# Cross attention of a fused decoder: one operation fewer on the masked scores, the normalised rows written by ScalarE, the low parts of the experts' weights subtracted on GpSimd

## The reference, cut to what matters

```python
def _layernorm(x, axis=-1, eps=1e-05):
    m = jnp.mean(x, axis=axis, keepdims=True)
    v = jnp.var(x, axis=axis, keepdims=True)
    return (x - m) / jnp.sqrt(v + eps)

def _L0_xattn_ref(hidden_states, memory_tokens, memory_mask):
    B, S, D = hidden_states.shape                         # 8, 256, 512
    scale = 1.0 / jnp.sqrt(D)
    scores = jnp.einsum('bsd,bmd->bsm', hidden_states, memory_tokens) * scale
    scores = jnp.where(memory_mask[:, None, :], scores, -1e+30)
    attn = jax.nn.softmax(scores, axis=-1)
    readout = jnp.einsum('bsm,bmd->bsd', attn, memory_tokens)
    valid_b = jnp.any(memory_mask, axis=-1)
    return jnp.where(valid_b[:, None, None], readout, jnp.zeros_like(readout))

x = _layernorm(x + _L0_xattn_ref(x, ctx_2048, mask_BxS2_bk0))
x = _layernorm(x + _L0_ffn_ref(x, Wg, Wu, Wd, ...))       # the experts, next stage
...
```

## Time and profile before

| what | value |
|---|---|
| median of 3 runs | 1967.81 us (1967.73 to 1971.22) |
| the profiled execution | 1972.95 us, span 1971.2 us |
| PE busy | 1732.7 us (88%) |
| DVE busy | 1378.8 us (70%) |
| ACT busy | 1038.9 us (53%) |
| POOL busy | 595.4 us (30%) |

### The profile page before, as it was taken

How to read it: one execution, slowest core, us unless ns; L and a number is a source line. 1 busy time by engine, 2 the same in 40 slices (tenths; PEclk the granted TensorE clock), 3 DMA queues, 4 the chain that set the end, 5 groups by cost and what they waited for, 6 DMA issues and landing times. The chain is left out here.

```text
span 1971.2 us, 32220 instructions
## 1 busy us (share of the span) xinstructions
PE 1732.7 (88%) x11756; PEld 1344.6 (68%) x11774; DVE 1378.8 (70%) x2884; ACT 1038.9 (53%) x1936; POOL 595.4 (30%) x550
## 2 busy tenths in 40 slices
PE   4489999788869999999999997999998899968875
PEld 2255666424558999999999996888886677734443
DVE  8478888587945566665665665465665799749996
ACT  3426666645415444444444443565565354469993
POOL 6133332033110001000000002223333498945642
PEclk9669999957979999999999998999998899979998
DMA  5398998062502122222212233223225375100001
GB/s 170 38 100 97 93 98 98 4 206 66 195 35 65 57 68 65 82 68 63 76 57 78 68 110 105 102 97 129 76 85 151 88 175 134 39 0 11 22 22 32
DMA packets 148480, 163.87 MB, mean 83 GB/s; under 512 B 46240, under 2 KB 100384, under 8 KB 146528
## 3 DMA queue, kind: packets, MB, share of 16 engines
q1 hardware_dynamic: 143076, 151.85, 34.2%
q10 hardware_dynamic: 5248, 9.96, 1.4%
HBM read 116.86 MB, written 19.48 MB: 69 GB/s over the span
## 5 line engine op out<-in xcount | busy, mean ns | idle before, releaser
L1659 ACT ACTIVATE f_gate<-f_gu 128x256 f32<-128x256 f32 x264 | 98.6, 382 | 270.8 <-PE f_gu L1523 190.6
L1800 DVE TENSOR_TENSOR f_hid<-f_gate,f_gu 128x256 f32<-128x256 f32 x264 | 108.1, 420 | 158.5 <-ACT f_gate L1659 155.0
L570 DVE TENSOR_REDUCE a_rowmax<-a_ring 128x2 f32<-128x512 f32 x256 | 164.9, 687 | 51.7 <-PE a_ring L652 49.2
L2825 PE MATMUL g_p<-e_kv,e_toep 128*128 128x288 f32 x640 | 163.3, 411 | 4.2 <-DVE e_planes L2884 4.2
L523 ACT ACTIVATE a_prob<-a_sT 128x1024 f32<-128x1024 f32 x128 | 130.6, 1027 | 47.8 <-PE a_sT L641 47.8
L1536 PE MATMUL f_gu<-f_lowh,f_bg 128*128 128x256 f32 x704 | 141.5, 283 | 5.2 <-POOL f_lowl L1441 5.0
L2825 PEld LDWEIGHTS g_p<-e_kv,e_toep 128*128 128x128 f32 x640 | 121.0, 193 | 36.2 <-issue 4.4
L1523 PE MATMUL f_gu<-f_xhi,f_wg 128*128 128x256 f32 x704 | 131.3, 284 | 0.0
L1523 PE MATMUL f_gu<-f_xhi,f_wu 128*128 128x256 f32 x704 | 130.4, 283 | 0.0
L1805 DVE TENSOR_TENSOR f_hl<-f_hid,f_hh 128x768 fp32r<-128x768 f32 (+2 forms) x90 | 84.5, 939 | 55.9 <-ACT f_hh L1707 54.8
L1536 PEld LDWEIGHTS f_gu<-f_lowh,f_bg 128*128 128x128 f32 x704 | 115.9, 191 | 9.7 <-POOL f_lowl L1441 5.2
(11 more groups left out here) (438 smaller groups left out, 4859.2 us busy)
## 6 DMA issues: line engine op xcount, KB each, us to landing
f_entry<-in_WdT SPq DMA_DIRECT2D x89, 256.0 KB, 2.8
d_staging<-in_w SPq DMA_DIRECT2D x16, 1024.0 KB, 6.1
a_qs<-a_hi SPq DMA_DIRECT2D x64, 128.0 KB, 7.4
a_ks<-a_hi SPq DMA_DIRECT2D x64, 128.0 KB, 6.1
e_toep<-lags SPq DMA_DIRECT2D x16, 512.0 KB, 4.2
f_entry<-in_Bg SPq DMA_DIRECT2D x89, 64.0 KB, 1.9
f_entry<-in_Bu SPq DMA_DIRECT2D x89, 64.0 KB, 2.0
cf<-in_xT SPq DMA_DIRECT2D x4, 1024.0 KB, 8.0
```

Of the source, the lines that this page charges most:

```text
L570: dve.tensor_reduce(rowmax[:, s % 2, :, e * SLOTS + j], ring[n % RING][:, :].rearrange("p (q t) -> p q t", t=T), AX.X, ALU.max, negate=Tru ...
L1659: act.activation(gate[:, i % 2, :], gu[n % 3][:, 0, :], ACT.Silu).then_inc(s_["gate_ready"], 1)
L1800: dve.tensor_tensor(hid[:, j, :], gate[:, i % 2, :], gu[n % 3][:, 1, :], ALU.mult).then_inc(s_["hid_ready"], 1)
L2825: last = pe.matmul(py[n % RING][:, 0:YS], toep[:, u, h % 2, (t - j) * P:(t - j + 1) * P], kv[:, h % 2, j, :, :].rearrange("p b c -> p (b c ...
```

## The change

Three edits in `cross_attention`:

- The scores: two VectorE operations (multiply the scaled scores by the mask, then add `shut`, which is 0 or -1e30) become one (scale, add `shut`). One `score_steps` count per tile instead of two, so TensorE's wait is `n - 1` instead of `2 * n - 2`.
- The normalised rows: `(y - mean) * root` on VectorE becomes `y * root + shift` as one activation on ScalarE. GpSimd makes the shift, minus mean times root, behind each inverse root, and signals it by the new semaphore `shift_ready`.
- The low parts of the pieces: the same subtraction, on GpSimd instead of VectorE, at the head of GpSimd's step.

```diff
 # GpSimd
                 for s in range(NT + 5):
+                    if s < NT:
+                        for n in pieces_of(s):
+                            pool.wait_ge(s_["w_high"], n + 1)
+                            pool.tensor_tensor(parts(n)[1], staged_piece(raw, n), parts(n)[0], ALU.subtract).then_inc(s_["w_low"], 1)
                     n = s - 4
                     if 0 <= n < NT:
                         inverse_roots(pool, stats, n, s_["var_ready"], n + 1, s_["root_ready"], keep)
+                        pool.wait_ge(s_["root_ready"], n + 1)
+                        pool.tensor_scalar(stats[:, n, 8:9], stats[:, n, 6:7], stats[:, n, 9:10], -1.0, ALU.mult, ALU.mult
+                                           ).then_inc(s_["shift_ready"], 1)
 # TensorE
-                            pe.wait_ge(s_["score_steps"], 2 * n - 2)
+                            pe.wait_ge(s_["score_steps"], n - 1)
 # ScalarE, behind the high parts of step s
+                    n = s - 4
+                    if 0 <= n < NT:
+                        act.wait_ge(s_["shift_ready"], n + 1)
+                        act.activation(row_of(rows, n), row_of(rows, n), ACT.Identity, bias=stats[:, n, 8:9],
+                                       scale=stats[:, n, 9:10]).then_inc(s_["x_ready"], 1)
 # VectorE
-                        sc.step(dve.scalar_tensor_tensor(score[:, n % 2, :], psc[n % 2][:, 0:T], D ** -0.5, mask[:, b % 2, :],
-                                                         ALU.mult, ALU.mult))
-                        sc.step(dve.tensor_tensor(score[:, n % 2, :], score[:, n % 2, :], shut[:, b % 2, :], ALU.add))
+                        sc.step(dve.scalar_tensor_tensor(score[:, n % 2, :], psc[n % 2][:, 0:T], D ** -0.5, shut[:, b % 2, :],
+                                                         ALU.mult, ALU.add))
-                    n = s - 4
-                    if 0 <= n < NT:
-                        y = row_of(rows, n)
-                        dve.wait_ge(s_["root_ready"], n + 1)
-                        dve.tensor_scalar(y, y, stats[:, n, 6:7], stats[:, n, 9:10], ALU.subtract, ALU.mult
-                                          ).then_inc(s_["x_ready"], 1)
-                    if s < NT:
-                        for n in pieces_of(s):
-                            dve.wait_ge(s_["w_high"], n + 1)
-                            dve.tensor_tensor(parts(n)[1], staged_piece(raw, n), parts(n)[0], ALU.subtract).then_inc(s_["w_low"], 1)
```

More of the change, by code:

```diff
@@ L1136, in cross_attention @@
         names = ("got_entry", "got_small", "mask_made", "mask_steps", "xf_done", "xf_ready", "sc_done", "score_steps", "max_ready",
-                 "exp_done", "pt_done", "pt_ready", "out_done", "added", "steps", "var_ready", "root_ready", "x_ready",
+                 "exp_done", "pt_done", "pt_ready", "out_done", "added", "steps", "var_ready", "root_ready", "shift_ready", "x_ready",
                  "w_high", "w_low", "got_taps", "skip_added", "taps_out")
```

## The result

| | median | runs |
|---|---|---|
| before | 1968.86 us | 4 (1967.73 to 1971.22) |
| changed | 1981.35 us | 4 (1978.8 to 1985.65) |

The ratio is 1.0064, with a 95% interval of 1.0043 to 1.0085: slower, as forecast, by 12.5 us where 7.5 were predicted. Timed again beside 15 runs of before it was 1978.86 against 1970.82, ratio 1.0042 (1.0028 to 1.0056), 8.0 us.

What follows compares the result with a forecast made beforehand. VectorE was taken to bound the kernel, and after the change a ScalarE-GpSimd ring of waits. Start -0.8, eleven steps 67.0 against 59.07 and tail +0.3 gave +7.4, rounded +7.5: 1975.3 us, range 1971 to 1981.

Steps and rivals of the forecast that it cites:

- The ring: In steps with pieces, ScalarE's normalisation awaits GpSimd's shift, queued behind low parts that await ScalarE's high parts: 5.47 or 7.18 us.
- Its length: Time between successive ScalarE exponentials: 5.47 us in a step with one piece of weights, 7.18 us with two.
- The sum: Cross-attention stage: gain at the start, longer steps and longer tail together add 7.4 us, rounded to +7.5.
- The eleven steps: From tile 4's exponential to tile 15's: seven one-piece and four two-piece steps, 67.0 us against 59.07.
- The tail: End of the stage: root to normalised row takes 1.70 us instead of 1.36, 0.3 more.
- The start: First steps, up to tile 4's exponential: it comes at 490.2 against 491.05, a gain of 0.8 us.
- The total: Whole kernel: +7.5 us, 1975.3 us on the base of the median 1967.81.
- Costs at nothing: DMA loads of pieces, ScalarE's stores, TensorE's wait for scores and TensorE's clock were each taken to add 0 us.
- TensorE becomes the bound: Rival: the shift comes in time, a step takes TensorE's 4.2 us, some -14 us, total 1954; chance 0.06.
- The one of slow GpSimd: Rival: VectorE slows GpSimd's root and shift, +12 us more, 1987; with low parts at 2.40, 1999; chance 0.10.
- stage of some 80 us: The prediction's figure for the stage's length, set beside about 33 us of work leaving VectorE.

Runs made afterwards that it cites:

- r2: Changed kernel with GpSimd making root and shift ahead of the low parts: 1958.24 us, ratio 0.9940, stage 79.7 us.
- r3: Changed kernel with ScalarE normalising tile s-5 instead of s-4 in step s: 1957.90 us, ratio 0.9941, stage 80.0 us.
- r7: Kernel before with only the low parts moved to GpSimd, ahead of the root: 1985.19 us, ratio 1.0079, stage 107.9 us.
- r5: Kernel before, unaltered, run again: ratio 1.0005, stage 93.7 us.
- r6: Kernel before with only the score edit (one VectorE operation instead of two): 1961.69 us, ratio 0.9960, stage 87.6 us.
- r8: Changed kernel with the low parts back on VectorE, at the end of its step: 1958.18 us, ratio 0.9941, stage 81.8 us.
- r10: Changed kernel with 20 one-column VectorE fills added behind its cross-attention loop: ratio 1.0036, stage 101.7 us.
- r4: Changed kernel with each low part split between GpSimd (columns 0 to 351) and VectorE (the rest): 1970.02 us, ratio 0.9998, stage 94.5 us.

## Why the prediction was right, point by point

**The ring.** It named the normalisation waiting for a shift queued behind low parts that wait for the high parts just in front of it. r2 and r3 break that order at its two ends and take 21 us out of the stage; r7 makes the same ring with another engine. That is shown.

**Its length.** Predicted 5.47 and 7.18 us; measured 5.42 and 7.08 to 7.19. The low part: 1.68 taken, 1.70 measured. The root: 0.55, and 0.55 measured, so the choice of the short end of the earlier trace rows was right. The reason fits too: the median of the roots is 0.78 us in the three traces with the normalisation beside them on VectorE (before, r5, r6) and 0.55 in the changed kernel and in r8. The shift was taken at 0.19 and is 0.26; shorter gaps made good for that (the root starts with none behind the low part, ScalarE 0.04 us behind the shift, and 0.08 was added for each).

**The sum.** It is to be compared with r5, because in the first trace of the kernel before TensorE ran at the low clock at both ends of the stage. The growth of the stage against r5 is 7.2 us, in three terms. The eleven steps gave 6.8 (65.90 against 59.09), where 7.9 were added up: I counted step 15 as a full ring, but no row copy follows there, and its period is 4.93 us; the rest is steps a few hundredths shorter than added. The tail gave 0.4, where I had 0.3. The start gave nothing, where I had a gain of 0.8: that was the term that I mis-sized. The prediction puts tile 4's exponential at 490.2, and it came at 490.14, but that is luck. The stage began 0.4 us later than before, and its first eight score matmuls took 2.58 us instead of 3.78. From the stage's start to that exponential, less those matmuls, it is 20.0 and 19.9 us in the two traces of before and 19.8 to 19.9 in the three of the changed kernel (r10 among them), a gain of 0.1. Where the gain went stands under the missed cost.

In the two first traces the stage grew by 4.2 us and not 7.4, because TensorE's clock lengthened the one of before at both ends (by 1.2 and some 1.7 us). In the changed kernel's tail TensorE had been idle 1.76 us ahead of the four readout matmuls, and they ran at full clock; r5 did so behind 2.49 us, so the shorter idle time is not shown to be the reason.

**The total.** +7.5 predicted, +12.5 and +8.0 measured in two comparisons, +5.8 in that of r10, with the fills. The stage gives 4.2 to 8.0 (100.9 to 101.7 against 96.7 or 93.7). The first two traces differ by 3.8 us outside it, of which 2.3 in the long-convolution stage (180.9 against 178.6). I had no term for that, and no run shows that the change causes it. The +12.5 also rests on four executions of each kernel: the median of before was 1968.86 us there, and 1970.32 to 1971.76 in the three comparisons with 11 to 17 of them. The hit on the total is sounder by +8.0 than by +12.5, and part of it is luck, as the start's missing gain and the steps' surplus cancelled.

**Costs at nothing.** TensorE's clock in the middle of the stage fell to 0.91 in one of the two windows above, and the ring hid it. That is right; the idle time was ahead of the scores, for want of the row copy. The stores and the loads of pieces never appear among the waits.

**A missed cost.** I asked whether VectorE would slow GpSimd, and not the reverse. It does: of the sixteen one-column multiplications (L1309) one took 1.74 us and the median 0.17, and a mask cast took up to 1.52 instead of 0.28. The wide operations that I called safe for having only one input include this cast and the scalar operation behind it. In the ring's steps VectorE had the time. In step 4 it had not:

```profile
479.76 1.84 POOL L1190 TENSOR_TENSOR f_ad<-c_raw,f_ad 128x768 fp32r<-128x768 f32 x1 [0.59 <-ACT f_ad L1267]
...
480.23 1.52 DVE L1286 CAST c_mask<-c_mask 128x256 f32<-128x256 uint8 x1
...
483.23 0.51 ACT L1254 ACTIVATE c_gap<-c_score,c_negmax 128x256 f32<-128x256 f32 x1 [3.06 <-DVE c_negmax L1302]
```

The cast, 1.24 us longer than alone, stands ahead of the masked scores, and ScalarE waits for their maximum. That is enough for the 0.7 us of gain that the start did not show; it is read from these rows, and no run tests it alone. In r2 the holds make steps of 6.3 us, which the next step gives back.

**The rivals.** "TensorE becomes the bound" was rejected for this order and is what happens in r2, whose other order takes its cause away (14 us under before written, 12.6 measured). The one of slow GpSimd is out: its low parts took 1.69 to 1.76 us. My "stage of some 80 us" was wrong (my own rows give 97); nothing hangs on it.

## What to carry to other kernels

An operation moved to an idle engine isn't free by its busy time: put it behind the short operations that others wait for, or ask for their result a step later. Before moving it, follow one full round of waits through the program order of both engines; when the moved work stands between a signal and the answer to that signal, its whole duration is added to every step. When after a change no engine is full, look for two engines that each wait for the other.

## What the runs showed of the hardware that I had not expected

- GpSimd and VectorE hold each other in both directions. A GpSimd subtraction of 704 columns (1.70 us) held VectorE's cast from uint8 (0.28 us) to 1.32 to 1.42 (1.52 beside one of 768 columns), a float32 operation with a constant (0.29) to 1.67 or 1.68, and a one-column multiplication of two SBUF operands (0.16) to 1.74. The other way, GpSimd's 352 columns took 1.28 us beside VectorE's two-input subtraction in r4, and 0.94 at best; in r8, where VectorE subtracts, the roots took up to 1.12 us and 0.55 at the median. VectorE's maximum over 256 columns and its masked score, with one PSUM and one SBUF input, stayed at their 0.42 us beside a subtraction. Held in the changed kernel (low parts from 527.62 to 531.04), and not held in r2:

```profile
528.06 1.42 DVE L1286 CAST c_mask<-c_mask 128x256 f32<-128x256 uint8 x1
529.51 1.68 DVE L1287 TENSOR_SCALAR c_shut<-c_mask 128x256 f32<-128x256 f32 x1
```
```profile
519.77 1.69 POOL L1196 TENSOR_TENSOR f_wu<-c_raw,f_wu 128x704 fp32r<-128x704 f32 x1 [2.00 <-ACT f_wu L1267]
...
520.25 0.42 DVE L1300 SCALAR_TENSOR_TENSOR c_score<-c_psc,c_shut 128x256 f32<-128x256 f32 x1
...
520.71 0.42 DVE L1302 TENSOR_REDUCE c_negmax<-c_score 128x1 f32<-128x256 f32 x1
```

  The Trainium skill (GPSIMD Engine Reference, Key points) names VectorE's instructions with two SBUF inputs or in a two-port mode as those that contend; these rows agree, if cast and scalar operation run in such a mode, which no row here shows by itself.
- After the same idle time of TensorE (2.48 and 2.49 us) its next four matmuls took 3.48 us in one execution and 1.98 in another. And behind the same 7.34 us at the start of the stage the first eight score matmuls took 2.53 to 3.78 us (2.59 and 3.78 in two traces of one kernel). A single trace doesn't tell what an idle time costs; 3 us of the kernel before hang on the two places.
